# A top-2 expert kernel with attention: its routing steps set later and further apart, and the rows of its tiles sent from body 4 on

## What is computed

```python
def reference(x, W_qkv, W_out, gate_w, gate_b, w1, b1, w2, b2):   # x: 8 x 512 x 128
    xn = _layernorm(x)
    # attention
    q, k, v = split(xn @ W_qkv)              # 32 heads of q, 16 of k and v, 64 wide
    scores = q @ k.T / sqrt(64) + slope * (key - query);  causal
    s = softmax(scores) @ v @ W_out
    # experts
    gate_logits = xn @ gate_w + gate_b
    topk_vals, topk_idx = jax.lax.top_k(gate_logits, 2)
    topk_w = jax.nn.softmax(topk_vals, axis=-1)
    comb = jnp.sum(onehot * topk_w[..., None], axis=2)
    h = gelu(einsum('btd,edf->ebtf', xn, w1) + b1)
    y = einsum('ebtf,efd->ebtd', h, w2) + b2
    g = silu(einsum('ebtd,bte->btd', y, comb))
    return x + s * g
```

## Time and profile before

| | us |
|---|---|
| time of the kernel, median of 3 runs | 1218.92 (1217.27 to 1220.55) |
| the profiled execution, its own time | 1220.46 |
| its span (first to last instruction) | 1218.7 |
| PE busy | 1128.5 (93%) |
| DVE busy | 990.2 (81%) |
| ACT busy | 936.7 (77%) |
| POOL busy | 887.8 (73%) |

### The profile page before, as it was taken

How to read it: one execution, slowest core, us unless ns; L and a number is a source line. 1 busy time by engine, 2 the same in 40 slices (tenths; PEclk the granted TensorE clock), 3 DMA queues, 4 the chain that set the end, 5 groups by cost and what they waited for, 6 DMA issues and landing times.

```text
span 1218.7 us, 51693 instructions
## 1 busy us (share of the span) xinstructions
PE 1128.5 (93%) x16970; PEld 833.0 (68%) x16970; DVE 990.2 (81%) x3099; ACT 936.7 (77%) x1835; POOL 887.8 (73%) x1064
## 2 busy tenths in 40 slices
PE   2668999999999999999998889999999999999996
PEld 1446666677777777777887657777777777777774
DVE  7787888878888888885776768888888888888883
ACT  4547887878888888887665578888888888888884
POOL 6059988888888888886000048888888888888895
PEclk8579999999999999999999999999999999999998
DMA  8425755655555555556335355555555555555554
GB/s 258 161 53 102 132 127 120 135 116 130 131 127 128 129 127 128 130 133 101 87 90 107 74 137 126 124 127 123 122 122 123 120 122 124 125 124 122 122 122 71
DMA packets 267956, 148.74 MB, mean 122 GB/s; under 512 B 173154, under 2 KB 256450, under 8 KB 267204
## 3 DMA queue, kind: packets, MB, share of 16 engines
q1 hardware_dynamic: 263476, 138.72, 51.3%
q0 software_dynamic: 4096, 8.40, 2.3%
q10 hardware_dynamic: 272, 0.13, 0.0%
HBM read 15.76 MB, written 16.78 MB: 27 GB/s over the span
## 4 chain that ended last, share of the span: by engine, by line
PE 64%; POOL 16%; issue 6%; DVE 4%; ACT 2%; DMA 1%; SPq 1%; POOLq 0%; ACTq 0%; DVEq 0%
POOL t_lo L812 11%; PE ps L965 10%; PE ps L937 7%; PE ps L871 7%; PE ps L872 6%; PE ps L873 6%; PE outs L997 6%; PE ps L969 5%; PE outs L1001 5%; PE outs L999 5%; PE ps L966 3%; PE ps L974 2%; ACT stage L1266 1%; POOL y_now L806 1%; PE outs L872 1%
## 5 line engine op out<-in xcount | busy, mean ns | idle before, releaser
L812 POOL TENSOR_TENSOR t_lo<-stage 128x512 f16<-128x512 f32 x640 | 652.2, 1038 | 120.4 <-ACT stage L1266 118.6
L1548 DVE CUSTOM_DVE_ANT_0 stage<-ps,kmask 128x512 bf16<-128x512 f32 (+3 forms) x1024 | 451.7, 487 | 111.0 <-PE ps L937 96.9
L1266 ACT ACTIVATE stage<-ps,slope 128x512 f32<-128x512 f32 (+1 forms) x768 | 440.4, 618 | 90.1 <-PE ps L974 77.9
L965 PE MATMUL ps<-q_st,k_st 128*128 128x256 f16 (+3 forms) x1024 | 299.7, 303 | 10.5 <-issue 5.0
L997 PE MATMUL outs<-v_sp,stage 128*128 128x65 f16 x2560 | 265.1, 195 | 9.6 <-POOL t_lo L812 7.8
L999 PE MATMUL outs<-v_sp,stage 128*128 128x64 f16 x2560 | 263.9, 194 | 0.0
L1001 PE MATMUL outs<-v_sp,t_lo 128*128 128x65 f16 x2560 | 263.8, 194 | 0.0
L997 PEld LDWEIGHTS outs<-v_sp,stage 128*128 128x128 bf16 x2560 | 235.5, 98 | 34.0 <-issue 14.5
L999 PEld LDWEIGHTS outs<-v_sp,stage 128*128 128x128 bf16 x2560 | 236.0, 99 | 0.0
L1001 PEld LDWEIGHTS outs<-v_sp,t_lo 128*128 128x128 f16 x2560 | 235.6, 98 | 0.0
L966 PE MATMUL ps<-q_st,k_st 128*128 128x128 f16 x1024 | 223.7, 218 | 0.0
(11 more groups left out here) (218 smaller groups left out, 2698.2 us busy)
## 6 DMA issues: line engine op xcount, KB each, us to landing
q_st<-stage SPq DMA_DIRECT2D x256, 128.0 KB, 2.4
k_st<-stage SPq DMA_DIRECT2D x128, 128.0 KB
q_st<-stage SPq DMA_DIRECT2D x256, 64.0 KB, 2.0
k_st<-stage SPq DMA_DIRECT2D x128, 64.0 KB
slot_y<-stage SPq DMA_DIRECT2D x40, 128.0 KB, 2.0
X<-in_L_attn_inputs SPq DMA_DIRECT2D x8, 512.0 KB, 7.5
slot_x<-att SPq DMA_DIRECT2D x2, 2048.0 KB, 8.9
wx_raw<-in_L_ffn_w SPq DMA_DIRECT2D x64, 64.0 KB
```

The source lines that it names most:

```text
L812: pool.tensor_tensor(t_lo[r], t_p[r], upper(t_p[r]), ALU.subtract).then_inc(s[f"lo{u % NG}"], 1)
L965: pe.matmul(d, k[:, 0, at], q[:, 0, seen], start=(c0 == 0), stop=False, skip_group_check=True)
L1266: e = act.activation(t_p[r][:, c0:c1], S_ps[u % 2][:, c0:c1], ACT.Exp, scale=slope[:, bass.ds(pair_index(n) * 2 * SLOTS + sl * 2 + h, 1)])
L1548: ins = dve.tensor_tensor_reduce(junk[h][:, c0:c0 + w], M_ps[h][:, c0:c0 + w], kmask[:, SEQ - w:SEQ], -1.0 / 1024, 3e38, ALU.add, ALU.min, ...
```

## The change

Nothing that is computed changes. Five things move.

- The routing steps on DVE. choose has four steps in place of six, the last with what were steps 3, 4 and 5; it stands behind Q0 of body 1, at the end of pass -1. route has ten: its steps 0 and 1 are in pass 0, 2 and 3 in pass 1, 4 and 5 in pass 2, 6 and 7 in pass 4, 8 in pass 5, and step 9 (the weights, formerly step 6) in pass 32, behind the last A1. Before, steps 0 to 5 were all in pass 0, and 6, 7 and 8 in passes 4, 6 and 8.
- ranks on PE goes from behind C0 of body 0 (pass -1) to behind S2 of body 0 (pass 0); keep_ranks from behind C1 of body 0 to behind E3 of body 0, and the exponential of the gap with it.
- On POOL wo_lo and the b2 conversions are spread over passes 0 to 3 (two, three, two, two) in place of passes 0 and 1 (five, four).
- The rows are sent from body 4 on (FIRST_SENT 2 to 4), with a second tile in bodies 6, 9, 12, 15 and 18 in place of 4, 7 and 10. The last sender is body 30 as before.
- A second tile's second expert is sent one body later, behind that body's own D1. With the larger TWICE the looped passes are 20 to 27.

```diff
-        FIRST_ONES = {"DVE": [("B1", 0), ("B3", 0), ("B5", 0), ("B7", 0), ("B9", 0), ("B11", 0),
-                              ("B3", 1), ("B5", 1), ("B7", 1), ("B9", 1), ("N0", 0), ("B11", 1),
-                              ("N0", 4), ("N0", 6), ("N0", 8)],
-                      "PE": [("C0", 0)], "ACT": [("C1", 0)],
...
-        CHOICES = 6
+        FIRST_ONES = {"DVE": [("B1", 0), ("B5", 0), ("B9", 0), ("Q0", 1), ("B9", 1), ("B11", 1), ("B5", 2), ("B9", 2), ("B5", 3), ("B9", 3),
+                              ("B5", 5), ("B9", 5), ("B5", 6), ("A1", HALF - 1)],
+                      "PE": [("S2", 0)], "ACT": [("E3", 0)],
+                      "POOL": [("L3", 0), ("L7", 0), ("L1", 1), ("L5", 1), ("L9", 1), ("L3", 2), ("L7", 2), ("L3", 3), ("L7", 3)]}
...
+        CHOICES = 4
...
-        FIRST_SENT, TWICE = 2, (4, 7, 10)
+        FIRST_SENT, TWICE = 4, (6, 9, 12, 15, 18)
...
-                for t, at, _ in sent_with(n, par):
+
+                sent = [(t, at) for t, at, _ in sent_with(n, par) if (k, at) != (1, UNROLL)]
+                if k == 1 and isinstance(n, int) and n - 1 in TWICE:
+                    sent.append(sent_with(n - 1, 0)[0][:2])
+                for t, at in sent:
```

More of the change, by code:

```diff
@@ L1075, in ranks @@
                 mm.then_inc(s["ranked"], 1)
-            enter_bodies("PE", {**tasks, "Y": ranks}, 0, HALF)
-            run_bodies(pe, "PE", tasks, 0, HALF)
+            enter_bodies("PE", tasks, 0, HALF)
+            run_bodies(pe, "PE", {**tasks, "Y": ranks}, 0, HALF)
             leave_bodies("PE", tasks, 0, HALF, late=LATE_O)
@@ L1523, in route @@
                 elif k == 6:
+                    small(dve.tensor_tensor(ended, block_no[:, :, :], end.unsqueeze(1).to_broadcast([P, NBLK, E]), ALU.is_ge))
+                elif k == 7:
+                    small(dve.tensor_reduce(blk_f[:, :], ended, AX_X, ALU.add))
+                    small(dve.tensor_scalar(blk_f[:, :], blk_f[:, :], E - 1.0, None, ALU.min))
+                elif k == 8:
+                    small(dve.tensor_tensor(eights[:, :, :], eights[:, :, :],
+                                            blk_f[0:1, :].rearrange("p (a b) -> p a b", b=WORD), ALU.mult))
+                    small(dve.tensor_reduce(word_f[:, :], eights[:, :, :], AX_X, ALU.add))
+                    dve.tensor_copy(blk_word[:, :], word_f[:, :]).then_inc(s["numbered"], 1)
+                else:
                     dve.wait_ge(s["topexp"], 1)
@@ L1527, in route @@
                     small(dve.tensor_tensor(top[:, 7, :], top[:, 6, :], top[:, 5, :], ALU.mult))
-                elif k == 7:
-                    small(dve.tensor_tensor(ended, block_no[:, :, :], end.unsqueeze(1).to_broadcast([P, NBLK, E]), ALU.is_ge))
-                    small(dve.tensor_reduce(blk_f[:, :], ended, AX_X, ALU.add))
-                    small(dve.tensor_scalar(blk_f[:, :], blk_f[:, :], E - 1.0, None, ALU.min))
-                else:
-                    small(dve.tensor_tensor(eights[:, :, :], eights[:, :, :],
-                                            blk_f[0:1, :].rearrange("p (a b) -> p a b", b=WORD), ALU.mult))
-                    small(dve.tensor_reduce(word_f[:, :], eights[:, :, :], AX_X, ALU.add))
-                    dve.tensor_copy(blk_word[:, :], word_f[:, :]).then_inc(s["numbered"], 1)
             def peaks(n, par, j):
@@ L1630, in _ @@
             run_bodies(dve, "DVE", {**tasks, "Y": lambda k: route(k - CHOICES)}, 0, HALF)
-            leave_bodies("DVE", tasks, 0, HALF, late=LATE_O)
+            leave_bodies("DVE", {**tasks, "Y": lambda k: route(k - CHOICES)}, 0, HALF, late=LATE_O)
             def parts(j, c, g):
```

13 lines of the change are left out of this document (5 added, 8 removed).

## The result

| | before | after |
|---|---|---|
| time, median of 20 runs each, us | 1220.22 (1216.64 to 1223.25) | 1222.66 (1219.51 to 1225.56) |
| span of the profiled execution | 1218.7 | 1220.8 |

The changed kernel takes 1.0024 times the time of before, 95% interval 1.0013 to 1.0036: some 3 us slower. 1208.0 was forecast. In the terms of the prediction that is within 0.3%, on the slow side. The forecast started from the median of three runs, 1218.92; that of 20 runs is 1220.22, so 1.3 of the 14.7 us between 1208.0 and 1222.66 lie in the value it started from.

The account below looks back on a forecast made before the run. TensorE was taken to set the pace, with VectorE and GpSimd only 12% to spare. Terms: -10.1 us to the mark of pass 11, -0.75 in passes 12 to 19, 0 at the drain, sum -10.9: 1208.0 us, range 1202 to 1215.

Parts of the forecast that it names:

- VectorE's debt is larger: Rival: steps 2 to 5 dearer by 3.4 us, clock loss at passes 1 and 4 another 3.4; 1214.8 us, chance 0.13.
- Pass -1: Three choose steps leave the path to the mark; 1.5 of about 2.8 us arrives, mark at 54.0 for 55.49.
- Pass 0: Route falls from six steps to two, choose and ranks come in: 25.9 us for 28.68, bounds 24 and 28.5.
- Pass 1: Steps 2 and 3 come in uncovered, 3.6 us: 20.15 us for 16.55, bounds +2.6 and +5.5.
- Passes 2 and 3: GpSimd's excess goes, steps 4 and 5 cost 1.5, clock 0.5: 32.2 us for 34.51, bounds 31 and 35.
- Pass 4: Steps 6 and 7, 2.70 us less 0.7 of cover, 2.0 over the floor: 17.1 us for 18.56.
- Passes 6 to 11: Two second tiles and no routing, 1.0 us over six passes of 15.10: 91.6 us.
- Passes 12 to 19: Written out saves 2.25 us, three second tiles cost 1.5: 0.75 less, bounds 2.2 less and 1.7 more.
- The drain: End of first half: step 9, about 0.8 us, hidden in VectorE's 0.88 idle before the experts' first split: 0.
- Slower than before: sends not covered: Rival: each of ten doubled passes delays TensorE by 1.26 us, low clock following; 1218 to 1226.6 us, chance 0.06.
- The spreading does not reach the marks: Rival: waits in passes 5 to 9 are steady engine exchange, 3.5 us of gain missing; 1214 us, chance 0.09.
- The start gains in earnest: Rival: pass 0 at its lower bound, pass 1 covers half its steps, 3.5 us more gained; 1204.5 us, 0.72 with forecast.

Follow-up runs that it names:

- run 8: Kernel after with only routing steps 2 to 8 at other places (2 and 3 in pass 0, 8 behind B11 of body 6); 1209.35 us, ratio 0.9909.
- run 3: Kernel before with step 8 behind B5 of body 10 (pass 9) in place of N0 of body 8; 1228.13 us in one run.
- run 4: Kernel after without the split: both DMAs of a second tile's second expert in its own body; 1230.98 us, ratio 1.0055.
- run 9: Kernel after with only steps 2 to 5 at the places of run 8, steps 6 to 8 left; 1217.31 us, ratio 0.9965.
- Run 10: Kernel after with only steps 7 and 8 moved, behind B11 of bodies 5 and 6; 1212.18 us, ratio 0.9922.
- run 12: Run 8 without the split of the sends (both DMAs of a second tile in its own body); 1215.07 us, ratio 0.9944.
- run 5: Kernel before with the new sends, split and spread GpSimd weight list, no routing step moved; 1218.22 us, ratio 0.9982.
- run 7: Kernel before's choice, ranks and steps 0 to 5, with the kernel after's sends and steps 6 to 9 at new places; 1211.43 us, ratio 0.9919.
- run 6: Kernel before with 20 bodies of the first half written out instead of 12, nothing else; 1222.06 us, ratio 1.0017.

## Why the prediction was wrong

**The step that failed is the price of the routing steps in pass 5 and, less and less surely, in passes 2 and 1.** I took durations of steps 2 to 5 and 8 at the places of the kernel before and gave them the same price at new ones. For step 8 that was 1.26, with 0.7 covered; it cost 6.9 (22.03 against 15.13 in run 8). Of the 9.2 us by which the mark of pass 11 missed its forecast, 6.0 are pass 5, that is this one product with the low clock behind TensorE's wait. The span missed its forecast by 13.0: 9.2 to the mark of pass 11, 0.7 in the rest of the first half's passes, 0.7 in the stretch of the experts, 2.7 in the first pass of the second half, less 0.3 behind it. I did see that a form took 0.43 and 1.28 by what GpSimd did and made a rival of it, but priced the rival at 0.85 an instruction, the length of about one GpSimd instruction, and only for steps 2 to 5. That is what the product of the earlier trace rows paid: it ended at 78.49, 0.28 behind the first of GpSimd's two low parts and well ahead of the second's end at 79.39. The product of step 8 is priced otherwise: in 13 of the 14 kernels it ended 0.05 to 0.06 behind the end of a run of GpSimd's without a pause, so its price is what is left of that run. Why it is passed over at the ends of single instructions, where larger ones get in, stays open. A smaller case stood in the trace of before, inside the first line of the earlier trace rows: the first instruction of step 6, at 149.40, took 1.36 and went over the end of one low part at 149.72. Looking for what GpSimd does at the new place in the trace of before would have shown four low parts and the copies of the next tile in one piece there.

The sentence of the Trainium skill that the prediction named (SBUF — State Buffer, "SBUF: two separate sides") has the exclusion last for a whole instruction of the one that came first. For the three products of pass 1 the rows agree (0.42 without, 1.10 to 1.28 with GpSimd at work, each ended 0.28 behind the GpSimd instruction that was ahead of it). For step 8 the measurement differs and decides: in the kernel after, in runs 3, 4 and 9 the product started and then lasted 4.80, 4.11, 4.79 and 4.78 us, over up to four whole low parts of 1.03 and what stood ahead of them.

Point by point:

- *Pass -1*: 53.81 for 54.0. Right.
- *Pass 0*: 24.01 for 25.9, at the lower bound. Choose moved behind the mark cost less than thought. The ranks came at 60.5 us and took 3.52, inside the forecast's 58 to 65 and next to the 3.75 of the earlier trace rows.
- *Pass 1*: 22.90 for 20.15. The three products took 3.53 where 0.43 each was possible, and the waits of 4.39 and 2.34 each brought a stretch at 1.2 GHz. Run 10 has 19.51 with the same code, so up to 3.4 of it is clock. In run 8, which does these steps ahead of the mark of pass 0, passes 0 and 1 together take 44.31 in place of 46.91; but run 10, which has them where the kernel after has them, takes 43.82. So what the places of steps 0 to 3 cost is not separated from the clock. TensorE's wait at this mark was 2.34, where 3 or more was forecast. The mark itself, 100.72 for 100.05, is near its forecast by luck: 2.1 us too many for the two passes ahead of it and 2.8 too few for this one.
- *Passes 2 and 3*: 34.27 for 32.2. Pass 3 was at the floor as forecast, pass 2 not: 19.14. Steps 4 and 5 stood there beside GpSimd at work (3.92 for 2.26), and run 8 with the same steps in pass 1 has 15.12. Of the 4.0 between them some 1.4 can be clock: run 12, with the steps of run 8 and a low clock behind the mark of pass 1, took 16.55. "Pass 2 over 18" was one of the signs of being wrong that the prediction named.
- *Pass 4*: 17.46 for 17.1. Right in size; behind B11 step 7 costs 1.2 less (runs 8 and 10).
- *Passes 6 to 11*: 91.70 for 91.6. Waits for t_lo of 0.27 where "under 0.6" was forecast, clock 1.00. The sum is right, and runs 5 and 12 confirm the sign of the sends' part; the size by run 12 is some 4 us for the split. Of the 6.4 us that these passes fell against before, the sends alone give 2.2 (run 5); the rest came when the routing steps were gone from them too (91.58 in run 7).
- *Passes 12 to 19*: 0.45 less for 0.75 less. Right. But "I add nothing for fetching more of it" is wrong elsewhere: by run 6 writing 8 more bodies out costs about 2 us, at the start of the second half. That is where the kernel after turned from 0.2 us ahead to 2.5 behind. This term had no rival, and the second half was called untouched.
- *The drain*: 0 for 0. Step 9 took 0.8 us as worked out, and the experts' first split came as soon as its input did.

The bounds for passes 4 and 5 together were 31 and 35; 39.5 was measured. The rival "VectorE's debt is larger" names the mechanism that decided, a VectorE instruction held up by GpSimd, but at 6.8 us, for steps 2 to 5, and without step 8; and a debt by count it is not, as run 8 with the same count shows. "Slower than before: sends not covered" was wrong in its cause. "The spreading does not reach the marks" did not come: passes 6 to 9 fell to 15.10 to 15.55. "The start gains in earnest" had pass 0 right, and pass 1 took it back. With the steps at other places the number of the forecast is met: run 8 gives 1209.35 for 1208.0. That is luck: its first half is faster than forecast (251.40 at pass 11 for 257.0) and pays for 2.9 us lost at the start of the second.

## What to carry to other kernels

In this kernel a small VectorE instruction with two inputs in SBUF, or a TENSOR_SCALAR from SBUF to SBUF, had no price of its own: look at what GpSimd does at the very place to which it goes, and put it where GpSimd waits or is about to. A sum of durations from the places of before is good only for instructions whose neighbours come along. When bodies are written out of a loop, look at the starts of all later stages too.
